# Turning the attended values inside the next batch's first heads, casting the keys' high parts on ScalarE, and sending the queries first

## The chip, the cores and the metric

The kernel runs on one NeuronCore of a Trainium2 chip. The metric is device time in microseconds. A core has TensorE (PE in the profile, its weight loads are PEld), VectorE (DVE), ScalarE (ACT), GpSimd (POOL) and SyncE (SP), which run their own instruction streams in order and meet through semaphores. Matmuls write PSUM, which POOL cannot reach; transposes in the kernel are made either by PE (a matmul against an identity) or by a DMA that SP issues.

## The reference

Tokens of 8 rows of 512 are embedded (three tables summed, then a layer norm), go through one attention layer and one mixture-of-experts layer with a residual around each. The attention is what matters here. For every batch row there are 16 heads; each has three branches: a causal one over compressed keys, one over 128 selected positions, and a window of 128.

```python
q = concatenate([qn, rope(qr)])                 # 32 + 64 wide, 16 heads
o1 = attn(q, k1, v1, causal)                    # latent keys and values
o2 = attn(q, rope(k_selected), v_selected)      # 128 kept positions
o3 = attn(q, rope(k_window), v_window, window)  # the last 128 positions
o  = gate[0] * o1 + gate[1] * o2 + gate[2] * o3
h  = h + concat_heads(o) @ Wproj
```

## The kernel before

The first 200 us embed the tokens, choose the positions and prepare weights; the last 65 us are the experts. Between lies the attention, eight batches of 16 heads. A query tile of a head is 128 positions, so a head has four units, t = 0 to 3. For one unit PE computes the scores of the three branches into one of two PSUM buffers S (`scores`), DVE adds the mask and takes the row maxima (`maxima`, L1029), ACT takes the exponentials (`probs`, L653), PE turns the probabilities into PSUM PT (`turn_probs`, L1402 and L1409), ACT copies them out as fp16 (`take_hi`, L665), DVE makes the rest of the rounding, also fp16 (`take_lo`, L1039), and PE multiplies by the values (`values`, L1424). All products in fp16 are made from a high and a low part, three matmuls for each. The scores run three units ahead of the values. The order on each engine is written out by hand, in a function `turn` on PE (L1441), DVE (L1130) and ACT (L676) that does one head.

Beside this, every head needs its query and keys. PE projects head h+2's query at the start of turn h and head h+3's keys at its end into the one PSUM bank X (`q_proj`, `k_proj`); ACT copies them to `qk` (`evac_q`, `evac_k`). The next use of X waits for that copy. POOL does one `cycle` (L546) a head: `prepare` (L538) waits for both copies, rotates query and key together (L437, L438, L440, L441), casts the key to fp16 (L469), takes its rest (L472), casts the query (L458), takes its rest (L461); then come the rest of the next head's values (`low_values`, L492, whose high part ACT casts in `high_values`, L642) and the sum of the three branches of the head before (`branch_sum`, L485 and L487), which goes to `o_b`. There is one `qparts` and one `kparts`. SP turns each by a DMA transpose into `qh` and `kh`, the keys first (`turn_keys` L317, `turn_queries` L326), when they are split and the scores that read the old ones are done. PE waits for both, of head h+1, ahead of the scores of unit t = 1 of turn h; these are head h+1's first.

The last two heads of a batch prepare the next batch's first two heads (the other order of POOL is at the end of its block, after `heads`). Between batches stands `behind`, on each engine (ACT L729, DVE L1175, PE L1493): the last value projections, the first three scores, and what is left of the batch before. For that PE waits for the last `branch_sum`, turns `o_b` in four groups of four 128 x 128 blocks into PT (`attended`, L1500), and ACT and DVE copy two groups each to `oT` (L594, L1168). The projection with `Wproj` (`project_rows`, L1429) and the residual (`half_residual`, L1124) then stand in units 1 and 2 of the next batch's heads 0 and 1 and use X; the next key projection waits for the residual. The last batch has no `behind`; its values are turned ahead of the experts. During the last batch POOL also normalises rows for the experts in every second cycle (L507 to L512).

Of the kernel before, what the change touches and what calls it, by code (L numbers as in the profile page):

```python
# [5 lines left out]
B, T, C = 8, 512, 64  # L6
P = 128
# [25 lines left out]
def tower(nc, d, out):  # L33
# [5 lines left out]
    with ctx:  # L39
# [217 lines left out]
        def _(sp):  # L257
# [94 lines left out]
            for hp in range(NH // 2 - 1):  # L352
                turn_keys(0, (B - 1) * NH + hp * 2 + 2)
                turn_queries(0, (B - 1) * NH + hp * 2 + 2)
                sp.wait_ge(s["xn_row"], hp + 2)
                sp.dma_start(xn_all[:, hp * NT * C:(hp + 1) * NT * C].rearrange("p (t c) -> p t c", t=NT), xn_b[:]).then_inc(s["xn_kept"], 16)
                turn_keys(1, (B - 1) * NH + hp * 2 + 3)
                turn_queries(1, (B - 1) * NH + hp * 2 + 3)
# [13 lines left out]
        def _(g):  # L372
# [90 lines left out]
            def split_key(par, b, hh, turned):  # L463
                H = b * NH + hh
                g.wait_ge(s["rope"], turned)
                g.nop(nofuse=True)
                g.wait_ge(s["k_turned"], H * 16 + 16)
                g.nop(nofuse=True)
                g.tensor_copy(kparts[:, 0, :, NOPE:P], kk[par][:, :, NOPE:P]).then_inc(s["k_high"], 1)  # L469
                g.wait_ge(s["k_high"], H + 1)  # L470
                g.nop(nofuse=True)
                g.tensor_tensor(kparts[:, 1, :, NOPE:P], kk[par][:, :, NOPE:P], kparts[:, 0, :, NOPE:P], ALU.subtract).then_inc(s["k_split"], 1)  # L472
# [65 lines left out]
            def prepare(par, b, hh, x):  # L538

                n = rope_count(b, hh, None)  # L540
                g.wait_ge(s["x_evac"], x + 2)
                rope(qk[par], rt9, cos9, sin9, n)
                split_key(par, b, hh, n)
                split_query(par, b, hh, n)

            def cycle(b, h, par, rows=None, add=True):  # L546
# [45 lines left out]
        def _(act):  # L592
# [44 lines left out]
            def evac_k(par, x, H=None):  # L637
                if H is not None:
                    act.wait_ge(s["k_split"], H)
                evac(kk[par][:, :, NOPE:P], X[:, 0:5 * HD].rearrange("p (t q) -> p t q", t=5), x)  # L640

            def high_values(par, b, hh):  # L642
                act.wait_ge(s["pv_done"], (b * NH + hh) * NT - 2)
                copy(vh[par][:, 0, :, 0:VD], vall[:, :, ds(hh * VD, VD)]).then_inc(s["v_high"], 1)
# [30 lines left out]

            def turn(b, h, xb, p, last, nxt=None, rows=None, more=True):  # L676
# [52 lines left out]
            def behind(b, nxt, U, first):  # L729

                def attended(c):
                    act.wait_ge(s["oT_psum"], (b - 1) * 4 + c + 1)
                    copy(oT[:, c, :], PT[:, 0:512]).then_inc(s["oT_act"], 1)
# [6 lines left out]
                if not first:  # L740
                    attended(0)
                probs(0, 0, b, U)
                lead(LEAD.index("kp2"), nxt, b * NH)
                if not first:
                    attended(2)
                probs(1, 1, b, U + 1)
                take_hi(0, 0, U)
                probs(2, 2, b, U + 2)
# [7 lines left out]
            def heads(b, rows=False):  # L756
                with act.Fori(0, NH // 2 - 2) as hp:
                    for p in range(2):
# [57 lines left out]
        def _(dve):  # L816
# [312 lines left out]

            def turn(b, H, p, last, nxt=None, rows=None, back=None):  # L1130

                U = H * NT
                for t in range(NT):
# [41 lines left out]
            def behind(b, U, first):  # L1175
                value(b, 7)
                if not first:
                    attended(b - 1, 1)
                maxima(0, 0, U)
                if not first:  # L1180
                    attended(b - 1, 3)
                maxima(1, 1, U + 1)
# [11 lines left out]
            def heads(b, rows=False):  # L1194
                for p in range(2):
                    turn(b, b * NH + p, p, 0, rows=0 if rows and p == 0 else None, back=b - 1 if b > 0 else None)
                with dve.Fori(1, NH // 2 - 1) as hp:
                    turn(b, b * NH + hp * 2, 0, 0, rows=hp if rows else None)
                    turn(b, b * NH + hp * 2 + 1, 1, 0)
# [51 lines left out]
        def _(pe):  # L1251
# [160 lines left out]
            def values(u, t, p, U, first):  # L1412
# [14 lines left out]
                last.then_inc(s["pv_done"], 1)  # L1427

            def project_rows(b, t, x):  # L1429

# [9 lines left out]

            def turn(h, H, xb, p, last, b=None, nxt=None, rows=None, back=None, more=True):  # L1441


                U = H * NT
                for t in range(NT):
                    u = p * NT + t
                    if last < 1 and t == 0:
                        q_proj(h + 2, xb + x_index(0, "qp"))
                    if back is not None and t in (1, 2):
                        project_rows(back, p * 2 + t - 1, xb + 1)  # L1450
                    if back is not None and t == 3:
                        pe.wait_ge(s["h_done"], back * 2 + p + 1)
# [40 lines left out]
            def behind(b, nxt, H, first):  # L1493


                def attended(c):
                    if c >= 2:
                        pe.wait_ge(s[["oT_act", "oT_dve"][c % 2]], (b - 1) * 2 + 1)
                    for t in range(NT):
                        last = tp(PT[:, (c % 2) * 512 + t * P:(c % 2) * 512 + (t + 1) * P], o_b[:, t, c * P:(c + 1) * P], ident)  # L1500
                    last.then_inc(s["oT_psum"], 1)

                for j in range(6, 9):
                    value(b, j)
                if not first:
                    pe.wait_ge(s["osum_done"], H + 2)
                    pe.wait_ge(s["pT_sb"], 2 * H * NT + 2)
                    attended(0)
                    attended(1)
                pe.wait_ge(s["v_act"], b * 5 + 5)  # L1510
# [4 lines left out]
                lead("kp2", b, nxt)  # L1515
                if not first:
                    attended(2)
                    attended(3)
                scores(1, 1, 0, H * NT + 1)
                scores(2, 2, 0, H * NT + 2)  # L1520
                if not first:
                    pe.wait_ge(s["oT_act"], b * 2)
                    pe.wait_ge(s["oT_dve"], b * 2)
                turn_probs(0, 0, H * NT)
# [11 lines left out]
            def heads(b, rows=False):  # L1536
                for p in range(2):
# [205 lines left out]
```

## Time and profile before

| | |
|---|---|
| median of 3 runs | 1754.34 us (1753.4 to 1754.41) |
| the profiled execution | 1754.28 us, span 1752.5 us |
| busy: PE, DVE, ACT, POOL | 1365.7, 1399.5, 1209.9, 1362.3 us |
| granted clock of TensorE, mean | 0.964 of full speed |
| DMA transposes | 128 of queries, 128 of keys |

The rest of the time of an engine is idle: waiting for a semaphore or for its next instruction. The share of busy time is an average over the whole span. In the views below a row of a timeline gives the start, the duration, the engine, the line, the operation, output and inputs by the program's names, the shape and the count merged into the row; in brackets stands how long the engine was idle just before and what ended that. Instructions that follow each other at once overlap by some hundredths of a microsecond.

### The profile page before, as it was taken

To read this page: it belongs to the slowest core of one execution; us is meant where nothing else is said; L and a number is where in the kernel's file an instruction comes from. 1 tells how busy PE (TensorE), PEld (TensorE's weight loads), DVE (VectorE), ACT (ScalarE), POOL (GpSimd) and SP (SyncE) were. 2 spreads that over 40 slices of the span, in tenths; PEclk is the share of its full clock that TensorE was granted. 3 is DMA by queue.
4 is the path that set the end of the run, shared out by engine and by line. 5 is a ranking of instruction groups with operands and counts; after the bars stand their busy time and mean duration, and the time that the engine had idled before them with its cause. 6 is when DMAs were issued, how large, how long until landed. Compare 5 with 4: busy or idle time off the path is not lost.

```text
span 1752.5 us, 61262 instructions
## 1 busy us (share of the span) xinstructions
PE 1365.7 (78%) x19368; PEld 1140.4 (65%) x19368; DVE 1399.5 (80%) x4989; ACT 1209.9 (69%) x3280; POOL 1362.3 (78%) x1680
## 2 busy tenths in 40 slices
PE   1042388889888988888888888888888888888788
PEld 0021277777777777777777777777777777777643
DVE  4756678888888888878887888878888888888835
ACT  0032178877787788778887788778877887777634
POOL 6775578977897789779987898789877997899510
PEclk9986599999999999999999999999999999999989
DMA  5110133223332323232233233332333332333200
GB/s 99 23 26 6 30 73 54 54 48 69 56 64 48 66 55 61 55 67 55 54 57 63 53 64 55 59 55 54 55 62 52 64 58 42 64 66 69 57 4 22
DMA packets 327657, 93.59 MB, mean 53 GB/s; under 512 B 321104, under 2 KB 323024, under 8 KB 327520
## 3 DMA queue, kind: packets, MB, share of 16 engines
q1 hardware_dynamic: 324448, 88.61, 27.2%
q0 software_dynamic: 3072, 3.15, 1.1%
q8 instruction: 85, 1.39, 0.3%
q14 instruction: 52, 0.43, 0.1%
HBM read 6.64 MB, written 1.05 MB: 4 GB/s over the span
## 4 chain that ended last, share of the span: by engine, by line
POOL 51%; issue 23%; DVE 10%; PE 9%; DMA 3%; POOLq 2%; ACT 2%; DVEq 0%; ACTq 0%; SPq 0%
POOL big L438 9%; POOL big L437 8%; POOL big L398 6%; POOL qk L440 5%; POOL qk L441 5%; POOL vh L492 4%; POOL kparts L469 4%; POOL qparts L458 4%; DVE S L1029 3%; POOL osum L485 2%; PE S L1377 2%; DMA kh<-kparts 2%; POOL o_b L487 2%; DVE big L1039 1%; POOL kparts L472 1%
## 5 line engine op out<-in xcount | busy, mean ns | idle before, releaser
L653 ACT ACTIVATE big<-S,negm 128x128 f32<-128x128 f32 (+3 forms) x1536 | 575.6, 448 | 196.2 <-DVE negm L1029 195.6
L1039 DVE SCALAR_TENSOR_TENSOR big<-PT,big 128x384 f16<-128x384 f32 (+3 forms) x1024 | 471.3, 499 | 17.1 <-ACT big L665 11.4
L665 ACT ACTIVATE big<-PT 128x384 f16<-128x384 f32 (+3 forms) x1024 | 417.3, 458 | 90.1 <-PE PT L1402 67.6
L1029 DVE CUSTOM_DVE_ANT_0 S<-S,mask_c,unscale 128x128 f32<-128x128 f32 (+3 forms) x512 | 284.7, 556 | 160.9 <-PE S L1377 157.3
L1377 PE MATMUL S<-k1T,qh 128*128 128x128 f16 (+3 forms) x1536 | 294.9, 301 | 141.0 <-DMA qh<-qparts 101.3
L1377 PE MATMUL S<-kh,qh 128*128 128x128 f16 (+1 forms) x3072 | 320.0, 241 | 0.0
L1424 PEld LDWEIGHTS O<-vh,big 128*128 128x128 f16 x8064 | 273.7, 96 | 22.9 <-issue 6.3
L1424 PE MATMUL O<-vh,big 128*128 128x33 f16 x8064 | 283.1, 178 | 4.4 <-issue 3.9
L437 POOL TENSOR_TENSOR big<-qk,cst 128x576 f32<-128x576 f32 (+2 forms) x144 | 182.5, 1267 | 104.9 <-ACT qk L594 103.1
L1377 PEld LDWEIGHTS S<-kh,qh 128*128 128x128 f16 x3072 | 227.3, 99 | 55.2
L1409 PE MATMUL PT<-cst,big 128*128 128x128 f32 x1408 | 244.5, 278 | 2.7 <-DVE big L1039 2.6
L1402 PE MATMUL PT<-cst,big 128*128 128x128 f32 x1280 | 230.7, 279 | 17.0 <-DVE big L1039 16.4
L1377 PEld LDWEIGHTS S<-k1T,qh 128*128 128x128 f16 x1536 | 116.0, 98 | 180.9 <-issue 126.5
L1029 DVE CUSTOM_DVE_ANT_0 S<-S,cst,kfix 128x256 f32<-128x256 f32 (+1 forms) x512 | 231.9, 453 | 0.0
L1029 DVE DVE_READ_ACCUMULATOR2_ANT negm<- 128x1 f32 x1536 | 215.4, 140 | 0.2
L1029 DVE CUSTOM_DVE_ANT_0 S<-S,mask_c,kfix 128x128 f32<-128x128 f32 x512 | 180.9, 353 | 0.1
L1409 PEld LDWEIGHTS PT<-cst,big 128*128 128x128 f32 x1408 | 164.4, 143 | 15.9 <-issue 10.0
L1402 PEld LDWEIGHTS PT<-cst,big 128*128 128x128 f32 x1280 | 151.4, 143 | 32.0 <-issue 14.7
L461 POOL TENSOR_TENSOR qparts<-qk,qparts 128x512 f16<-128x512 f32 x128 | 148.2, 1158 | 18.6
L594 ACT ACTIVATE qk<-X 128x480 f32<-128x480 f32 (+1 forms) x256 | 151.8, 593 | 14.5 <-PE X L1324 11.3
L438 POOL TENSOR_TENSOR big<-qk,big 128x576 f32<-128x576 f32 x112 | 157.8, 1409 | 0.0
L472 POOL TENSOR_TENSOR kparts<-qk,kparts 128x480 f16<-128x480 f32 x128 | 140.5, 1097 | 18.6
(296 smaller groups left out, 2092.0 us busy)
## 6 DMA issues: line engine op xcount, KB each, us to landing
lat_b<-lat_all SPq DMA_DIRECT2D x8, 448.0 KB, 3.1
qh<-qparts SPq DMA_TRANSPOSE x128, 3.1
kh<-kparts SPq DMA_TRANSPOSE x128, 3.5
xnT_all<-xnT_b SPq DMA_DIRECT2D x14, 128.0 KB, 2.5
xn_b<-xn_all SPq DMA_DIRECT2D x8, 128.0 KB, 2.8
xnT_b<-xnT_all SPq DMA_DIRECT2D x8, 128.0 KB, 2.7
out_dram<-h_all SPq DMA_DIRECT2D x8, 128.0 KB, 2.0
xn_all<-xn_b SPq DMA_DIRECT2D x7, 128.0 KB, 2.0
```

Of the source, the lines that this page charges most:

```text
L437: g.tensor_tensor(tmp[:, 0], v, cos, ALU.mult)
L438: g.tensor_tensor(tmp[:, 1], v, sin, ALU.mult).then_inc(s["rope_t"], 1)
L472: g.tensor_tensor(kparts[:, 1, :, NOPE:P], kk[par][:, :, NOPE:P], kparts[:, 0, :, NOPE:P], ALU.subtract).then_inc(s["k_split"], 1)
L594: return nc.scalar.activation(dst, src, ACT.Copy)
L653: last = nc.scalar.activation(pr[par][:, lo:lo + n], S[par][:, lo:lo + n], ACT.Exp, bias=negm[par][:, k:k + 1], scale=-1.0)
L665: last = nc.scalar.activation(pT[par][:, 0, lo:lo + n], PT[:, lo:lo + n], ACT.Copy, scale=PSCALE)
L1029: last = v.tensor_tensor_reduce(out=z, in0=z, in1=m, scale=unscale[:] if k == 0 else kfix[:], scalar=3.0e38, op0=ALU.add, op1=ALU.min, acc ...
L1039: v.scalar_tensor_tensor(pT[par][:, 1, lo:lo + n], PT[:, lo:lo + n], PSCALE, pT[par][:, 0, lo:lo + n], ALU.mult, ALU.subtract).then_inc(s[ ...
L1377: last = mm(z[:, lo:lo + n], qh[par][:, c, t * P:(t + 1) * P], keys[:, a, :], start=(c + a == 0), stop=(c == 1))
L1402: last = tp(PT[:, lo:lo + P], src[:, lo:lo + P], ident)
L1409: last = tp(PT[:, lo:lo + P], src[:, lo:lo + P], ident)
L1424: last = mm(o, w[:, c, blocks[i] * P:(blocks[i] + 1) * P], vh[p][:, a, v0 + i, :], start=(j == 0), stop=(j == len(parts) - 1))
```

## The change

Three things are altered.

1. The attended values are no longer turned in `behind`. PE turns group c in units 1 and 2 of the next batch's heads 0 and 1 into X (`attended_rows`), ACT copies the even groups there, after `take_hi` of unit 1, and DVE the odd ones in unit 2; the next key projection waits for DVE's copy. The projection and the residual move on by two heads, to heads 2 and 3. These heads are now written out on PE and DVE (four instead of two), and two on ACT (none before). POOL's last addition of `branch_sum` waits, from the second batch on, until the batch before is turned.
2. In `prepare` POOL no longer casts the key; ACT does (`high_key`), in unit 2 of the turn, after `take_hi`. It waits for POOL's rotation, and POOL's rest of the key waits for the cast. The four heads prepared at the change of batches (two each time) keep the old way. `high_values` on ACT moves from unit 2 to unit 1.
3. POOL splits the query before the key, and SP sends the queries' transpose before the keys'.

```diff
@@ sync
                     for par in range(2):
+                        turn_queries(par, b * NH + hp * 2 + (par + 2))
                         turn_keys(par, b * NH + hp * 2 + (par + 2))
-                        turn_queries(par, b * NH + hp * 2 + (par + 2))
@@ gpsimd
             def branch_sum(par, b, hh):
...
+                if b > 0:
+                    g.nop(nofuse=True)
+                    g.wait_ge(s["oT_psum"], b * 4)
+                    g.nop(nofuse=True)
                 g.tensor_tensor(o_b[:, :, ds(hh * VD, VD)], osum[:], obr[par][:, :, 2, :], ALU.add).then_inc(s["osum_done"], 1)
...
                 rope(qk[par], rt9, cos9, sin9, n)
-                split_key(par, b, hh, n)
                 split_query(par, b, hh, n)
+                low_key(par, b, hh)
@@ scalar
+            def high_key(par, b, hh):
+                H = b * NH + hh
+                act.wait_ge(s["rope"], b * (NH + 2) + hh + 3)
+                act.wait_ge(s["k_turned"], H * 16 + 16)
+                copy(kparts[:, 0, :, NOPE:P], kk[par][:, :, NOPE:P]).then_inc(s["k_high"], 1)
...
-                    if t == 2 and last < 2:
+                    if t == 1 and last < 2:
                         high_values(1 - p, b, h + 1)
...
                         take_hi(u + 1, (t + 1) % NT, U + t + 1, rows)
+                    if back is not None and t == 1:
+                        act.wait_ge(s["oT_psum"], back * 4 + 2 * p + 1)
+                        copy(oT[:, 2 * p, :], X[:, 0:512]).then_inc(s["oT_act"], 1)
+                    if t == 2 and last < 1:
+                        high_key(p, b, h + 2)
@@ vector
-                    if back is not None and t == 2:
+                    if back is not None and t == 2 and early:
+                        dve.wait_ge(s["oT_psum"], back * 4 + 2 * p + 2)
+                        v.tensor_copy(oT[:, 2 * p + 1, :], X[:, 0:512]).then_inc(s["oT_dve"], 1)
+                    if back is not None and t == 2 and not early:
                         half_residual(back, p)
@@ tensor
+            def attended_rows(b, c, x):
+                if c == 0:
+                    pe.wait_ge(s["osum_done"], (b + 1) * NH + 2)
+                if c % 2 == 0:
+                    x_wait(x)
+                if c % 2 == 1:
+                    pe.wait_ge(s["oT_act"], b * 2 + c // 2 + 1)
+                for t in range(NT):
+                    last = tp(X[:, t * P:(t + 1) * P], o_b[:, t, c * P:(c + 1) * P], ident)
+                last.then_inc(s["oT_psum"], 1)
...
-                    if back is not None and t in (1, 2):
+                    if back is not None and early and t in (1, 2):
+                        attended_rows(back, p * 2 + t - 1, xb + 1)
+                    if back is not None and early and t == 3:
+                        pe.wait_ge(s["oT_dve"], back * 2 + p + 1)
+                    if back is not None and not early and t in (1, 2):
                         project_rows(back, p * 2 + t - 1, xb + 1)
...
-                for p in range(2):
-                    turn(p, b * NH + p, xbase(b) + p * 2, p, 0, rows=0 if rows and p == 1 else None, back=b - 1 if b > 0 else None)
-                with pe.Fori(1, NH // 2 - 2) as hp:
+                for h in range(4):
+                    turn(h, b * NH + h, xbase(b) + h * 2, h % 2, 0, rows=h // 2 if rows and h % 2 == 1 else None,
+                         back=b - 1 if b > 0 else None, early=h < 2)
+                with pe.Fori(2, NH // 2 - 2) as hp:
```

The three `attended` functions of `behind` and their calls and waits go.

## Rows read from the trace of the kernel before

**Rows 1.** The page, part 1: busy us, share of span, instructions.

```profile
PE 1365.7 (78%) x19368; PEld 1140.4 (65%) x19368; DVE 1399.5 (80%) x4989; ACT 1209.9 (69%) x3280; POOL 1362.3 (78%) x1680
```

**Rows 2.** Waits, whole span: who waited for whom, us, times, longest.

```profile
POOL big L437 <- ACT qk L594: 103.1, 65, 14.9
PE S L1377 <- DMA qh<-qparts: 101.3, 69, 3.6
```

**Rows 3.** Timeline of POOL, steady heads of the second batch.

```profile
514.07 1.40 POOL L437 TENSOR_TENSOR big<-qk,cst 128x576 f32<-128x576 f32 x1 [0.25 <-ACT qk L594]
...
518.73 0.58 POOL L469 CAST kparts<-qk 128x480 f16<-128x480 f32 x1 [0.27 <-POOL qk L441]
519.45 1.10 POOL L472 TENSOR_TENSOR kparts<-qk,kparts 128x480 f16<-128x480 f32 x1
520.50 0.61 POOL L458 CAST qparts<-qk 128x512 f16<-128x512 f32 x1
521.25 1.16 POOL L461 TENSOR_TENSOR qparts<-qk,qparts 128x512 f16<-128x512 f32 x1
...
524.13 1.40 POOL L437 TENSOR_TENSOR big<-qk,cst 128x576 f32<-128x576 f32 x1
...
534.50 1.40 POOL L437 TENSOR_TENSOR big<-qk,cst 128x576 f32<-128x576 f32 x1 [0.30 <-ACT qk L594]
```

**Rows 4.** Timelines of SP and PE there; last, landing times of all key transposes.

```profile
520.78 1.32 SPq L323 DMA_TRANSPOSE kh<-kparts  x1
522.55 1.23 SPq L332 DMA_TRANSPOSE qh<-qparts  x1
...
525.89 0.34 PE L1377 MATMUL S<-k1T,qh 128*128 128x128 f16 x3 [1.69 <-DMA qh<-qparts]
...
DMA to landing us min/median/max: 3.3/3.5/5.8
```

**Rows 5.** Timeline of POOL: third batch, heads 4 and 14; last batch, a pair.

```profile
609.92 1.40 POOL L437 TENSOR_TENSOR big<-qk,cst 128x576 f32<-128x576 f32 x1 [1.02 <-ACT qk L594]
...
712.07 1.40 POOL L437 TENSOR_TENSOR big<-qk,cst 128x576 f32<-128x576 f32 x1 [0.23 <-ACT qk L594]
...
1510.68 1.41 POOL L437 TENSOR_TENSOR big<-qk,cst 128x576 f32<-128x576 f32 x1 [1.74 <-ACT qk L594]
...
1533.41 1.39 POOL L437 TENSOR_TENSOR big<-qk,cst 128x576 f32<-128x576 f32 x1
```

**Rows 6.** Timeline of ACT, the steady stretch of rows 3.

```profile
516.66 0.88 ACT L665 ACTIVATE big<-PT 128x384 f16<-128x384 f32 x2
...
518.22 0.45 ACT L594 ACTIVATE vh<-vall 128x288 f16 x1
518.62 0.98 ACT L665 ACTIVATE big<-PT 128x512 f16<-128x512 f32 x2
...
522.37 1.20 ACT L653 ACTIVATE big<-S,negm 128x384 f32<-128x384 f32 x3 [0.79 <-DVE negm L1029]
```

**Rows 7.** Timelines of PE, DVE, SP and POOL, from second to third batch.

```profile
579.42 1.09 PE L1500 MATMUL PT<-cst,o_b 128*128 128x128 f32 x8 [1.36 <-POOL o_b L487]
...
587.84 1.08 PE L1437 MATMUL X<-wproj,oT 128*128 128x64 f32 x8
588.76 0.33 PE L1377 MATMUL S<-k1T,qh 128*128 128x128 f16 x3
...
580.55 0.69 DVE L1168 COPY oT<-PT 128x512 f32<-128x512 f32 x1 [2.35 <-PE PT L1500]
...
585.17 1.33 SPq L323 DMA_TRANSPOSE kh<-kparts  x1
...
587.77 1.41 POOL L437 TENSOR_TENSOR big<-qk,cst 128x576 f32<-128x576 f32 x1 [2.86 <-ACT qk L594]
...
598.83 1.41 POOL L437 TENSOR_TENSOR big<-qk,cst 128x576 f32<-128x576 f32 x1 [2.10 <-ACT qk L594]
```

More of the change, by code:

```diff
@@ L542, in prepare @@
                 rope(qk[par], rt9, cos9, sin9, n)
-                split_key(par, b, hh, n)
                 split_query(par, b, hh, n)
+                low_key(par, b, hh)
             def cycle(b, h, par, rows=None, add=True):
@@ L674, in take_hi, with turn @@
                     last.then_inc(s["pT_hi"], 1)
-            def turn(b, h, xb, p, last, nxt=None, rows=None, more=True):
+            def turn(b, h, xb, p, last, nxt=None, rows=None, more=True, back=None):
                 H = b * NH + h
@@ L729, in behind @@
             def behind(b, nxt, U, first):
-                def attended(c):
-                    act.wait_ge(s["oT_psum"], (b - 1) * 4 + c + 1)
-                    copy(oT[:, c, :], PT[:, 0:512]).then_inc(s["oT_act"], 1)
                 value(b, 6)
@@ L739, in behind @@
                 copy(vh[0][:, 0, :, 0:VD], vall[:, :, 0:VD]).then_inc(s["v_high"], 1)
-                if not first:
-                    attended(0)
                 probs(0, 0, b, U)
                 lead(LEAD.index("kp2"), nxt, b * NH)
-                if not first:
-                    attended(2)
                 probs(1, 1, b, U + 1)
@@ L756, in heads @@
             def heads(b, rows=False):
-                with act.Fori(0, NH // 2 - 2) as hp:
+                for p in range(2):
+                    turn(b, p, xbase(b) + p * 2, p, 0, rows=0 if rows and p == 1 else None, back=b - 1 if b > 0 else None)
+                with act.Fori(1, NH // 2 - 2) as hp:
                     for p in range(2):
@@ L1128, in half_residual, with turn @@
                 v.tensor_tensor(hb, X[:, i * 2 * C:(i + 1) * 2 * C], hb, ALU.add).then_inc(s["h_done"], 1)
-            def turn(b, H, p, last, nxt=None, rows=None, back=None):
+            def turn(b, H, p, last, nxt=None, rows=None, back=None, early=False):
                 U = H * NT
@@ L1176, in behind @@
                 value(b, 7)
-                if not first:
-                    attended(b - 1, 1)
                 maxima(0, 0, U)
-                if not first:
-                    attended(b - 1, 3)
                 maxima(1, 1, U + 1)
@@ L1194, in heads @@
             def heads(b, rows=False):
-                for p in range(2):
-                    turn(b, b * NH + p, p, 0, rows=0 if rows and p == 0 else None, back=b - 1 if b > 0 else None)
-                with dve.Fori(1, NH // 2 - 1) as hp:
+                for h in range(4):
+                    turn(b, b * NH + h, h % 2, 0, rows=h // 2 if rows and h % 2 == 0 else None,
+                         back=b - 1 if b > 0 else None, early=h < 2)
+                with dve.Fori(2, NH // 2 - 1) as hp:
                     turn(b, b * NH + hp * 2, 0, 0, rows=hp if rows else None)
@@ L1439, in project_rows, with turn @@
                     last.then_inc(s["attn_psum"], 1)
-            def turn(h, H, xb, p, last, b=None, nxt=None, rows=None, back=None, more=True):
+            def turn(h, H, xb, p, last, b=None, nxt=None, rows=None, back=None, early=False, more=True):
                 U = H * NT
@@ L1448, in turn @@
                         q_proj(h + 2, xb + x_index(0, "qp"))
-                    if back is not None and t in (1, 2):
+                    if back is not None and early and t in (1, 2):
[3 more added lines that the diff above has]
+                    if back is not None and not early and t in (1, 2):
                         project_rows(back, p * 2 + t - 1, xb + 1)
-                    if back is not None and t == 3:
+                    if back is not None and not early and t == 3:
                         pe.wait_ge(s["h_done"], back * 2 + p + 1)
@@ L1493, in behind @@
             def behind(b, nxt, H, first):
[L1496 to L1501, printed above, removed]
                 for j in range(6, 9):
                     value(b, j)
[L1505 to L1509, printed above, removed]
                 pe.wait_ge(s["v_act"], b * 5 + 5)
@@ L1515, in behind @@
                 lead("kp2", b, nxt)
-                if not first:
-                    attended(2)
-                    attended(3)
                 scores(1, 1, 0, H * NT + 1)
                 scores(2, 2, 0, H * NT + 2)
-                if not first:
-                    pe.wait_ge(s["oT_act"], b * 2)
-                    pe.wait_ge(s["oT_dve"], b * 2)
                 turn_probs(0, 0, H * NT)
@@ L1536, in heads @@
             def heads(b, rows=False):
-                for p in range(2):
-                    turn(p, b * NH + p, xbase(b) + p * 2, p, 0, rows=0 if rows and p == 1 else None, back=b - 1 if b > 0 else None)
-                with pe.Fori(1, NH // 2 - 2) as hp:
+                for h in range(4):
+                    turn(h, b * NH + h, xbase(b) + h * 2, h % 2, 0, rows=h // 2 if rows and h % 2 == 1 else None,
+                         back=b - 1 if b > 0 else None, early=h < 2)
+                with pe.Fori(2, NH // 2 - 2) as hp:
                     for p in range(2):
```

6 lines of the change are left out of this document (4 added, 2 removed).

## The prediction

> **What bounds the kernel now.** The page gives four engines about the same busy share: DVE 1399.5 us, PE 1365.7, POOL 1362.3, ACT 1209.9 [rows 1]. So shares don't say who waits for whom; the table of waits comes next. Its two entries that matter are POOL's first multiply of the rotation (L437) waiting for the evacuation of the next queries by ACT, and PE's scores waiting for the transposed queries [rows 2]. Each waits for the other's product, 65 and 69 times. That is a ring, not a pipeline behind one engine.
>
> The timelines of one undisturbed stretch give the ring its lengths. POOL starts on head 12's query and key at 514.07 after an idle 0.25 (it waited for ACT), and on head 14's at 534.50, again after a wait of 0.30 [rows 3]. PE starts the first scores of head 12 at 525.89, having idled 1.69 for the landing of the queries [rows 4]. So
>
> - L, from POOL's start to the scores: 525.89 - 514.07 = 11.82 us (rotation 4.66, key cast and rest, query cast and rest, transposition, landing);
> - R, from the scores to POOL's start two heads later, through PE, DVE and ACT in that order: 534.50 - 525.89 = 8.61 us.
>
> L + R = 20.43 for two heads, 10.2 a head. The stretch from 609.92 to 712.07 [rows 5] has ten heads: 10.2 each. POOL alone could do a head in 524.13 - 514.07 = 10.06 [rows 3]; it is close behind, but not first. About 12 of 16 heads in each of seven batches (84) run like this. In the last batch POOL has the normalisation too, and two heads take 1533.41 - 1510.68 = 22.73 [rows 5]: there POOL sets the pace.
>
> The Trainium skill (Perfetto Trace Analysis, section Identifying the Most-Contended Engine) says to take the engine with the highest occupancy as the bottleneck and to optimise it first. Relieving POOL is in that spirit. The trace speaks against it outside the last batch; what the rule would give is rival A.
>
> **The change, part by part.** All sums are against the profiled execution's own 1754.28 us (span 1752.5 and 1.8 around it), which is 0.06 under the median shown.
>
> *1. Key cast to ACT, queries first: L.* On POOL one head loses 519.45 - 518.73 = 0.72 [rows 3]. L changes otherwise. Now: cast of the key at 4.66, its rest, cast of the query, its rest until 522.41, that is 8.34, issue at 8.48 [rows 3, 4]. After: query cast at 4.66, its rest 0.75 later, ready at 4.66 + 0.75 + 1.16 = 6.57; key rest 1.10 more: 7.67. SP issues the query at 6.57 + 0.23 (520.78 stands 0.23 behind the end of L472), is held 1.23 by it, and takes 0.14 for the next, so the key goes out at 8.17, not 7.9. Its landing takes 3.5 (median) where the queries' took 3.1 or so (525.89 - 522.55 = 3.34 with PE's 0.24) [rows 3, 4]. 8.17 + 3.5 + 0.24 = 11.91: L grows by 0.09. What is late next is the key, the longer transpose, in the queries' place. Bounds: -0.1 (its shortest landing, 3.3) to +0.3 (the two transposes, now 1.4 apart instead of 1.8, hinder each other). I take +0.09.
>
> The high part must be there when POOL reaches it. ACT ends its 512-column copy at 519.60 [rows 6], which is 5.53 after POOL's start and after the rotation (4.4); the cast, about 0.58 by the copies of 288 and 512 columns, ends at 6.2, POOL needs it at 6.6. Covered by 0.4; where something delays ACT at this place by more, POOL, the key's transpose and the scores are late by the rest.
>
> *2. What ACT gets: R.* The added 0.58 stands before the exponentials of a unit; behind these are the next key's evacuation, a copy and the exponentials that end R. ACT idles 0.79 just there, for DVE [rows 6], so it is hidden, by 0.2. The value cast (0.45) moves ahead of the copy at 516.66, before which ACT had no idle time in this head [rows 6]. The copy is what DVE and then PE's next transposes wait for. Bounds: 0 (it falls into idle time) and 0.45. I take 0.2, about half. Evacuating the key 0.6 later makes PE's query projection late, but evacuation of the queries waits for the exponentials anyway.
>
> Steady heads: (0.09 + 0.2)/2 = 0.145 a head, since L and R are shared by two heads; 84 x 0.145 = **+12.2 us**. Bounds (-0.1 + 0)/2 and (0.3 + 0.45)/2: -4 to +31.
>
> *3. Attended values out of the gap between batches.* Now PE idles 1.36 for POOL's last sum and turns 8 blocks (1.09) before the first scores [rows 7]; these go 1.4 us earlier. But the first scores of head 1 stand at 588.76, and its key was issued at 585.17, 3.59 before them [rows 7] (a transpose and PE's 0.24), on a chain that runs on POOL alone from the last heads on. It isn't shortened; two sums with the added wait and its no-operations (0.1 each, from the 0.27 ahead of L469 [rows 3]) lengthen it by 0.2. So the 1.4 us end as idle time at 588.8. What the gap gives is POOL's start on head 2, now after 2.86 idle [rows 7]; nobody waits for it first.
>
> Then the added work lands in R. A quarter of the projection (1.08) or a turning of 4 blocks (0.55, half of the 1.09) [rows 7] stands in each of units 1 and 2 of a head; the one in unit 2 is inside R, with the wait of the key projection behind it. From 588.76 to 598.83 is 10.07, against 8.61: the projection costs 1.46 there, its 1.08 and 0.38 of the wait for DVE's addition [rows 7]. With the turning I take 0.55 + 0.87 = 1.42, as DVE then copies for 0.69 [rows 7] where it adds 128 columns now (bounds of that wait 0.38 and 1.07). With S for first scores, P for POOL's start, both by head:
> before: S1 588.76, P3 598.83, P4 609.92, S3 = P3 + 11.82 = 610.65, P5 619.26, S4 621.74, P6 630.35, S5 = P5 + 11.82 = 631.08.
> after: S1 588.96, P3 = + 10.03 = 598.99, S2 = P3 + 0.39 (one turning of 0.55 in place of the 1.08 with which it was 0.92) = 599.38, P4 609.41, S3 = P3 + 11.82 = 610.81, P5 = + 10.07 = 620.88, S4 = P5 + 0.92 = 621.80, P6 = 631.87, S5 = P5 + 11.82 = 632.70.
> Both strands of the ring are 1.5 to 1.6 late: four heads now pay in R where two did. 7 x 1.55 = **+10.9 us**; bounds 0 (projection halves fall into PE's waits) and +17 (they also make the key's cast late). The wait that the sums get for all turning done is over by 6 us when they come, and costs its no-operations only, which POOL has room for.
>
> *4. Last batch.* POOL's 22.73 becomes 22.73 - 2 x 0.72 + 2 x 0.1 = 21.49; six pairs: -7.4. The ring (20.43 and the rows' work) comes near, so I take **-6 us** (-8 to -1).
>
> *5. Longer straight code* on PE, DVE and ACT means more loading of instructions; landings of up to 5.8 against 3.5 [rows 4] show transposes that something holds up. 0 taken, +7 at most.
>
> Sum 12.2 + 10.9 - 6 = +17.1: 1754.3 + 17.1 = **1771 us**.
>
> **Rivals.**
> A. *POOL sets the pace everywhere.* For it: 10.06 of 10.2, and 1362 us busy. Against it: POOL's waits on ACT, 0.25 and 0.30 in [rows 3]. Price -0.62 x 84 = -52, with part 4 -59: 1695. Below 10.06 nothing follows unless L or R shortens. 7%.
> B. *The gap's gain is kept* (faster): the first scores 1.4 us earlier pass through because the key of head 1 comes in time or heads 2 and 3 absorb the projection in PE's 1.69 idle. Its place is S1; it decides if S1 moves by over 0.7. -10, with part 4 -16, steady heads unchanged: 1738. Against it: the 3.59 us from 585.17 [rows 7]. 13%.
> C. *Nothing to be seen*: steady heads at 0, half of part 3, and part 4 take each other up: 1754. 12%.
> D. *ACT becomes the bound*: the value cast costs its whole 0.45, key casts are late: +31 + 11 - 6: 1790. 13%.
> The forecast with its own range (1759 to 1783) has 55%.
>
> A difference of over 0.2% (3.5 us) can be told from none: faster 20%, same 12%, slower 68%. The range, 1740 to 1790, takes in B nearly and D, and leaves A out.
>
> **What will show it.** Right: PE's scores wait for kh<-kparts instead of qh<-qparts; POOL's wait on ACT (now 103.1) grows by some 0.6 a head while its busy time falls by 60 us; ten steady heads take 103 to 104 us; the first scores of head 1 still follow the key's landing; POOL's start on heads 5 and 6 comes later behind S1 by 1.5; last-batch pairs near 21.5. Wrong: POOL without idle time before L437, ten heads in under 101, or S1 more than a microsecond nearer to the start of its batch.

## The result and the profile after

| | before | after |
|---|---|---|
| median | 1754.38 us | 1807.03 us (4 runs, 1801.75 to 1811.11) |
| profiled execution, span | 1754.28, 1752.5 us | 1811.11, 1809.0 us |
| mean granted clock | 0.964 | 0.953 |

The ratio is 1.030 (1.0267 to 1.0334). The forecast was 1771 us, range 1740 to 1790: the sign is right, but the loss foreseen is a third of what came, and the time lies above the range. Some executions of most kernels lie 40 to 50 us above the rest and ratios leave these out on both sides; the one profile here that is of such an execution (the run with half of the turnings left out) spends its added time at the lower clock behind 1707 us, after the attention, so that its heads can be compared.

The first part of the page after. POOL has 62.5 us less work than in [rows 1], the kernel takes 53 us more.

```profile
PE 1415.4 (78%) x19368; PEld 1160.5 (64%) x19368; DVE 1407.7 (78%) x4989; ACT 1262.0 (70%) x3392; POOL 1299.8 (72%) x1568
```

Waits, whole span (us, times, longest), beside [rows 2]: the keys stand in the queries' place in PE's wait, POOL waits more for ACT, and there is a new wait of POOL for the cast key.

```profile
POOL big L437 <- ACT qk L602: 164.6, 114, 14.9
PE S L1390 <- DMA kh<-kparts: 102.8, 95, 3.7
POOL kparts L476 <- ACT kparts L602: 60.6, 34, 5.2
```

POOL's timeline in a steady stretch of the fifth batch, for [rows 3, 5]. Four heads take 1100.31 - 1058.61 = 41.70, 10.42 each, where they took 10.2. POOL's time that became free is idle time ahead of L437: 0.98 a head, where [rows 3] has 0.25, nothing and 0.30.

```profile
1058.61 1.41 POOL L437 TENSOR_TENSOR big<-qk,cst 128x576 f32<-128x576 f32 x1 [0.97 <-ACT qk L602]
...
1063.27 0.61 POOL L458 CAST qparts<-qk 128x512 f16<-128x512 f32 x1 [0.28 <-POOL qk L441]
1064.03 1.16 POOL L461 TENSOR_TENSOR qparts<-qk,qparts 128x512 f16<-128x512 f32 x1
1065.15 1.11 POOL L476 TENSOR_TENSOR kparts<-qk,kparts 128x480 f16<-128x480 f32 x1
...
1079.45 1.40 POOL L437 TENSOR_TENSOR big<-qk,cst 128x576 f32<-128x576 f32 x1 [0.98 <-ACT qk L602]
...
1100.31 1.41 POOL L437 TENSOR_TENSOR big<-qk,cst 128x576 f32<-128x576 f32 x1 [0.98 <-ACT qk L602]
```

SP and PE there, for [rows 4]: the key goes out at 1066.80, 8.19 behind POOL's start (8.17 was worked out), and the scores start at 1070.28, 11.67 behind it. PE's scores follow the key's landing.

```profile
1065.42 1.23 SPq L332 DMA_TRANSPOSE qh<-qparts  x1
...
1066.80 1.37 SPq L323 DMA_TRANSPOSE kh<-kparts  x1
...
1070.28 0.34 PE L1390 MATMUL S<-k1T,qh 128*128 128x128 f16 x3 [0.82 <-DMA kh<-kparts]
```

The first heads of the third batch, for [rows 7], all engines. PE turns group 0 early, idles 2.14 for head 1's key and starts its scores (S1) at 602.28. The second turning waits 0.70 for ACT's copy, the key projection for DVE's. POOL has the query ready by 606 but waits 5.07 for ACT's key cast, which stands behind a copy ahead of which ACT itself idles 2.93.

```profile
599.51 0.63 PE L1451 MATMUL X<-cst,o_b 128*128 128x128 f32 x4 [0.47 <-ACT qk L602]
...
602.28 0.41 PE L1390 MATMUL S<-k1T,qh 128*128 128x128 f16 x3 [2.14 <-DMA kh<-kparts]
...
605.74 1.12 PE L1451 MATMUL X<-cst,o_b 128*128 128x128 f32 x4 [0.70 <-ACT oT L602]
...
609.40 0.98 ACT L679 ACTIVATE big<-PT 128x512 f16<-128x512 f32 x2 [2.93 <-issue]
...
610.26 0.61 ACT L602 ACTIVATE kparts<-qk 128x480 f16<-128x480 f32 x1
...
610.52 0.50 PE L1346 MATMUL X<-wkw,xh 128*128 128x96 f16 x8 [0.42 <-DVE oT L1160]
...
611.01 1.10 POOL L476 TENSOR_TENSOR kparts<-qk,kparts 128x480 f16<-128x480 f32 x1 [5.07 <-ACT kparts L602]
...
615.40 1.41 POOL L437 TENSOR_TENSOR big<-qk,cst 128x576 f32<-128x576 f32 x1 [2.63 <-ACT qk L602]
```

POOL starts on head 3 at 615.40, 13.12 behind S1; before it was 10.07 [rows 7], predicted 10.03. The stretches show the other half of why. Columns: stretch, length, busy time (instructions) of PE, its loads, DVE, ACT, POOL, granted clock, DMA share, GB/s. Just behind the idle time TensorE runs at its lower level, 1.2 GHz, for 7 us.

```profile
599.40:602.20 2.80, 0.63 (x4) 0.42 (x4) 1.26 (x6) 2.20 (x6) 2.75 (x2) 1.00 0.83 195
602.20:609.20 7.00, 6.22 (x48) 5.68 (x49) 2.67 (x11) 2.25 (x6) 3.32 (x5) 0.51 0.43 110
609.20:615.30 6.10, 5.68 (x98) 4.97 (x97) 5.23 (x19) 5.22 (x14) 1.77 (x2) 1.00 0.37 57
```

Where the time lies, by the ends of ACT's evacuation of the queries, mean of batches 1 to 6 (counted from 0), in us:

| stretch of a batch | before | after | only part 1 | parts 2 and 3 |
|---|---|---|---|---|
| heads 0 to 2 | 29.4 | 27.8 | 27.8 | 29.3 |
| heads 2 to 8 | 65.0 | 72.9 | 71.3 | 64.9 |
| heads 8 to 14 | 61.2 | 62.7 | 61.2 | 62.5 |
| head 14 to the next batch | 24.2 | 25.5 | 24.4 | 24.7 |

Most of the loss is in heads 2 to 8, and part 1 brings it. Parts 2 and 3 cost heads 8 to 14 1.3 a batch and heads 2 to 8 nothing: there even the kernel before takes 10.8 a head and not 10.2, so the plain ring of the prediction holds for some 8 heads of a batch and not for 12.

### The profile page after: what moved, and what is told of

Read it like the earlier page. It is cut to its first block and busy times, and to the rows that moved or that the text cites. A ratio compares the mean times of both kernels' runs of the same rounds, so it can differ in the third digit from the quotient of the medians.

```text
span 1809.0 us, 60454 instructions
## 1 busy us (share of the span) xinstructions
PE 1415.4 (78%) x19368; PEld 1160.5 (64%) x19368; DVE 1407.7 (78%) x4989; ACT 1262.0 (70%) x3392; POOL 1299.8 (72%) x1568
## 5 line engine op out<-in xcount | busy, mean ns | idle before, releaser
L1390 PE MATMUL S<-kh,qh 128*128 128x128 f16 (+1 forms) x3072 | 325.5, 243 | 0.0
L437 POOL TENSOR_TENSOR big<-qk,cst 128x576 f32<-128x576 f32 (+2 forms) x144 | 182.6, 1268 | 164.9 <-ACT qk L602 164.6
L1437 PEld LDWEIGHTS O<-vh,big 128*128 128x128 f16 x8064 | 278.0, 96 | 19.4 <-issue 6.3
L1390 PEld LDWEIGHTS S<-kh,qh 128*128 128x128 f16 x3072 | 231.3, 100 | 56.3
L1415 PE MATMUL PT<-cst,big 128*128 128x128 f32 x1280 | 238.2, 286 | 25.8 <-DVE big L1052 24.7
L1422 PE MATMUL PT<-cst,big 128*128 128x128 f32 x1408 | 248.3, 281 | 2.2 <-DVE big L1052 1.4
L1415 PEld LDWEIGHTS PT<-cst,big 128*128 128x128 f32 x1280 | 153.4, 146 | 56.1 <-DVE big L1052 31.7
L1422 PEld LDWEIGHTS PT<-cst,big 128*128 128x128 f32 x1408 | 166.9, 145 | 22.6 <-issue 12.1
```

The lines of the kernel that those rows point to most:

```text
L437: g.tensor_tensor(tmp[:, 0], v, cos, ALU.mult)
L1390: last = mm(z[:, lo:lo + n], qh[par][:, c, t * P:(t + 1) * P], keys[:, a, :], start=(c + a == 0), stop=(c == 1))
L1415: last = tp(PT[:, lo:lo + P], src[:, lo:lo + P], ident)
L1422: last = tp(PT[:, lo:lo + P], src[:, lo:lo + P], ident)
L1437: last = mm(o, w[:, c, blocks[i] * P:(blocks[i] + 1) * P], vh[p][:, a, v0 + i, :], start=(j == 0), stop=(j == len(parts) - 1))
```

## Experiments

Ratios are to the kernel before, with their 95% intervals; 0.001 is 1.75 us. L (from POOL's start on a head to its first scores) and R (from there to POOL's start two heads on) are the prediction's; here both are read from the ends of ACT's evacuation of the queries (POOL starts some 0.3 behind).

### Only the attended values moved

```diff
  # kernel before, with the change's part 1 alone; POOL casts the key, keys sent first
-                if not first: attended(...)        # behind, on PE, ACT and DVE
...
+                        attended_rows(back, p * 2 + t - 1, xb + 1)
```

> The kernel before with part 1 alone: attended values turned in heads 0 and 1, projection in heads 2 and 3, the loops written out as in the changed kernel; POOL casts the key, keys go first, value cast in unit 2. Theory 1 (TensorE's clock): the early scores leave PE idle by 2 us ahead of head 1's first scores, the granted clock halves there for 3.4 or 6.8 us in most batches, and that is what the heads 2 to 7 lose: most of the loss is here, 1785 to 1795 us, with ten or more stretches at half clock between 400 and 1550 us. Theory 2 (the key cast on ACT comes late): without the cast on ACT the heads 2 to 7 of a batch lose only the 1.6 us of my sum: 1762 to 1768 us, and few stretches at half clock. Steady heads stay at 10.2 us under both.

1787.69 us, ratio 1.0192 (1.0146 to 1.0239): +33.7 us. The steady heads are as before. Heads 0 to 2 gain 1.6 us a batch, heads 2 to 8 lose 6.3. The time is the one that goes with theory 1, but the attention has 8 stretches at half clock, not ten or more, and the next run shows that they are not the bulk of the loss.

### The same, with PE kept busy while it waits for head 1's key

```diff
+                            if back is not None and early and p == 0:
+                                for _ in range(18):
+                                    mm(O[:, 416:512], k1T[:, 0, 0:P], k1T[:, 0, 0:96], start=True, stop=True)
                             pe.wait_ge(s["k_turned"], H * 16 + 48)
```

> The kernel attended with 18 matmuls of 96 columns that nobody reads, written to unused columns of O, on PE in head 0 ahead of its wait for head 1's key (1.5 to 1.9 us of idle time there in attended). They add work and shorten nothing. Theory 1 (the idle stretch halves the granted clock and that costs the time): no stretch at half clock behind the change of batches any more (seven batches, 3.4 to 10.2 us each in attended), heads 2 to 8 come down from 70 to 72 us to 65 to 67: 1760 to 1770 us. Rival (projection and turning in R alone cost it, the clock is a consequence): 1785 to 1795 us, as attended or a little over.

1782.01 us, 1.0165 (1.0140 to 1.0191): 4.7 us less by the ratios, though the intervals overlap; that is nearer to the rival's time than to theory 1's. The idle time ahead of S1 falls to 1.11, and the stretch behind it keeps the full clock. One batch of each kernel, first with only the values moved, behind a gap of 1.87 (S1 at 958.5):

```profile
958.40:961.80 3.40, 2.85 (x30) 2.68 (x30) 1.62 (x8) 1.18 (x3) 2.98 (x5) 0.50 0.50 148
```

and with the added matmuls (S1 at 589.38):

```profile
589.38 0.34 PE L1388 MATMUL S<-k1T,qh 128*128 128x128 f16 x3 [1.11 <-DMA kh<-kparts]
```

```profile
592.00:599.00 7.00, 6.14 (x96) 5.43 (x97) 4.72 (x19) 4.56 (x13) 3.48 (x4) 1.00 0.47 87
```

So the clock may be part of it, some 5 us, but no more: with all seven of these idle times at 0.96 to 1.39 and none of them followed by half clock, 29 of the 34 us stay.

### The first heads written out, nothing moved

```diff
-                for p in range(2):
-                    turn(p, b * NH + p, xbase(b) + p * 2, p, 0, ...)
-                with pe.Fori(1, NH // 2 - 2) as hp:
+                for h in range(4):
+                    turn(h, b * NH + h, xbase(b) + h * 2, h % 2, 0, ...)
+                with pe.Fori(2, NH // 2 - 2) as hp:
...  # the same two heads more on DVE, and heads 0 and 1 on ACT
```

> The kernel before with heads 2 and 3 written out on PE and DVE and heads 0 and 1 on ACT, and nothing moved: 18 or so more loads of instructions. If instruction loads that hit the transposes are a large part of the loss of attended: 1765 to 1775 us, with waits of PE of 2 to 3.5 us and half clock behind them. If they are the small term of my step 5 (0 taken, 7 at most): 1752 to 1761 us.

1761.39 us, 1.0029 (1.0014 to 1.0045): +5.1 us for straight code alone. The page counts 103 instruction loads on the DMA queues instead of 85. In one stretch of the DMA view (822 to 832 us) such a load stands beside a query transpose that lands after 5.4 us, and PE idles 3.91, 2.2 us more than in [rows 4]. Queue, packets, MB; issues with the median landing; then PE:

```profile
q8 instruction: 1, 0.02, 0.7%
...
kh<-kparts SPq DMA_TRANSPOSE x2, 3.5
qh<-qparts SPq DMA_TRANSPOSE x1, 5.4
```

```profile
828.24 0.34 PE L1380 MATMUL S<-k1T,qh 128*128 128x128 f16 x3 [3.91 <-DMA qh<-qparts]
```

No run isolates the load, but the fourteen traces bear it out. Of their transposes issued between 200 and 1700 us, 2724 have no instruction load that begins within 3 us of their issue, and 28 of these land over 1 us behind the median of their kind (3.1 and 3.5); of the 858 that have one, 311 do. All 28 have a load that begins later, before they land. The Trainium skill (Runtime: NRT & Kernel Launch, Instruction fetch mechanics) calls the cost of such a load mostly hidden and full unrolling preferred; this kernel measures +5.1 us for it.

### Half of the turnings left out

```diff
-                    if back is not None and early and t in (1, 2):
-                        attended_rows(back, p * 2 + t - 1, xb + 1)
+                    if back is not None and early and t == 1:
+                        attended_rows(back, p * 2, xb + 1)
...  # DVE copies the turning that is there a second time
```

> Only the attended values are moved, as in the run 'attended' (1787.7 us), but the odd groups c = 1 and 3 are not turned: their 8 turnings a batch are left out, and VectorE copies the even group a second time. With them goes PE's wait in unit 2 for ScalarE's copy out of X. Theory (the step R from a head's first scores to POOL's start two heads on grew through the second turning, 0.55 us, and its wait of about 0.87 us for ScalarE, where the prediction had counted one copy only): R of the two turning heads falls from about 11.4 to about 10 us, 1.4 us a batch or a little more on each strand, 7 batches: about 1777 us. Rival (the moved work costs nothing there, the loss is instruction loads and the lower clock, which this leaves as they are): 1785 to 1789 us.

1776.73 us, 1.0122 (1.0104 to 1.0140): 12.3 us less than with all of them, with intervals apart. The same place in both, head 2's first scores to the evacuation of head 4's queries, PE and ACT. First with all turnings: 602.99 to 614.53, R = 11.54.

```profile
602.99 0.33 PE L1388 MATMUL S<-k1T,qh 128*128 128x128 f16 x3
...
605.50 0.62 ACT L602 ACTIVATE oT<-X 128x512 f32<-128x512 f32 x1
...
606.18 0.66 PE L1449 MATMUL X<-cst,o_b 128*128 128x128 f32 x4 [0.87 <-ACT oT L602]
...
606.67 0.49 PE L1388 MATMUL S<-k1T,qh 128*128 128x256 f16 x3
...
609.73 0.50 PE L1344 MATMUL X<-wkw,xh 128*128 128x96 f16 x8 [0.86 <-DVE oT L1158]
...
613.92 0.61 ACT L602 ACTIVATE qk<-X 128x512 f32<-128x512 f32 x1
```

With the second left out: 602.83 to 612.85, R = 10.02.

```profile
602.83 0.33 PE L1389 MATMUL S<-k1T,qh 128*128 128x128 f16 x3
...
605.00 0.49 PE L1389 MATMUL S<-k1T,qh 128*128 128x256 f16 x3
...
608.05 0.50 PE L1345 MATMUL X<-wkw,xh 128*128 128x96 f16 x8 [0.78 <-DVE oT L1159]
...
612.24 0.61 ACT L602 ACTIVATE qk<-X 128x512 f32<-128x512 f32 x1
```

The second turning costs 1.5 us of R: 606.67 - 602.99 = 3.68 against 605.00 - 602.83 = 2.17 to the next scores, of which 0.87 is the wait for ACT to empty X.

### The keys' part: cast by ACT, queries first, nothing else moved

```diff
+                    if t == 2 and last < 1:
+                        high_key(p, b, h + 2)
...
-                    if t == 2 and last < 2:
+                    if t == 1 and last < 2:
                         high_values(1 - p, b, h + 1)
```

> The kernel before with parts 2 and 3 alone: key cast on ACT in unit 2, value cast in unit 1, queries split and sent first; attended values stay between the batches. Both theories: steady heads at 10.42 us as in the changed kernel (R longer by 0.47, L shorter by 0.1). Theory 1: no idle 2 us ahead of head 1's first scores, so few stretches at half clock, 84 heads x 0.22 = +18 and a last batch unchanged: 1768 to 1775 us. Theory 2: key casts late in the heads behind the change of batches, because ACT does the projection's neighbours there: 1780 to 1795 us.

1768.57 us, 1.0100 (1.0061 to 1.0140). L is 11.81 (before 11.90), R 9.02 (8.50), medians over the steady heads.

### The same, with the cast of the values left in unit 2

> As keys, but the value cast of ACT stays in unit 2. If the value cast ahead of the copy of unit 1 is what lengthens R (my step 2), R comes back to 8.5 to 8.6, steady heads take 10.15 to 10.2 and the kernel 1745 to 1756 us, now with a shorter L. If it is the key cast ahead of the exponentials of unit 2, R stays at 9.0 and the time is that of keys.

1748.22 us, 0.9965 (0.9952 to 0.9977), faster than before; L 11.83, R 8.51. Measured again:

> The same kernel as keys_hv2, measured again in more rounds, since it stood only 0.35% under the kernel before. If that was the edit, 1746 to 1750 us; if it was chance, within 0.1% of the kernel before, 1753 to 1756 us.

1750.36 us, 0.9968 (0.9955 to 0.9981). The gain is small and real, and in the profiles it shows in the last batch only, where POOL sets the pace: from head 0's to head 15's evacuation that takes 173.6 and 173.3 us in the two profiles against 178.1, while batches 1 to 6 together are no shorter (1080.7 and 1082.4 against 1078.7). One line takes the gain to a loss of 1%. Its way through the engines, a steady head of the third batch in each, counted from the first scores: first with the values cast in unit 2.

```profile
674.57 0.34 PE L1389 MATMUL S<-k1T,qh 128*128 128x128 f16 x3 [1.13 <-DMA kh<-kparts]
...
675.67 0.87 ACT L675 ACTIVATE big<-PT 128x384 f16<-128x384 f32 x2
...
676.21 1.01 DVE L1051 SCALAR_TENSOR_TENSOR big<-PT,big 128x384 f16<-128x384 f32 x2
...
676.94 0.60 PE L1414 MATMUL PT<-cst,big 128*128 128x128 f32 x4
...
677.63 0.98 ACT L675 ACTIVATE big<-PT 128x512 f16<-128x512 f32 x2
...
682.46 0.61 ACT L598 ACTIVATE qk<-X 128x512 f32<-128x512 f32 x1
```

Cast in unit 1:

```profile
678.32 0.34 PE L1389 MATMUL S<-k1T,qh 128*128 128x128 f16 x3 [1.05 <-DMA kh<-kparts]
...
679.46 0.45 ACT L598 ACTIVATE vh<-vall 128x288 f16 x1
...
679.79 0.88 ACT L675 ACTIVATE big<-PT 128x384 f16<-128x384 f32 x2
...
680.32 1.02 DVE L1051 SCALAR_TENSOR_TENSOR big<-PT,big 128x384 f16<-128x384 f32 x2 [0.22 <-ACT big L675]
...
680.93 0.66 PE L1414 MATMUL PT<-cst,big 128*128 128x128 f32 x4
...
681.69 0.98 ACT L675 ACTIVATE big<-PT 128x512 f16<-128x512 f32 x2 [0.24 <-PE PT L1414]
...
686.58 0.61 ACT L598 ACTIVATE qk<-X 128x512 f32<-128x512 f32 x1
```

ACT's copy starts 1.47 behind the scores instead of 1.10, DVE's 2.00 (with a wait of 0.22 for it) instead of 1.64, PE's next transposes 2.61 instead of 2.37, ACT's next copy 3.37 instead of 3.06 (now waiting for PE), and the queries' evacuation 8.26 instead of 7.89. The cast goes round PE and DVE once and comes back to ACT as idle time. This head shows 0.37 of it; over the steady heads the median R grows by 0.51.

### Only the cast of the values moved

> The kernel before with one line moved: ScalarE casts the next head's values in unit 1 instead of unit 2. Theory (this alone lengthens R by its whole 0.5 us, as keys against keys_hv2 suggests: R 9.02 against 8.51): 84 heads x 0.25 = +21 us, about 1775 us. Rival (it costs only where ScalarE has the key's cast as well): R 8.5, 1754 to 1757 us.

1765.28 us, 1.0052 (1.0029 to 1.0076); R 8.64. Neither expectation is right: alone it costs R 0.14, with the key's cast behind it 0.5. The profiles show a reason, idle time of ACT ahead of the copy that the cast now precedes. In the kernel before, ACT idled 0.3 to 0.4 there in 18 of 42 steady heads (heads 6 to 11 of the first seven batches), as in this one; with the key's cast on ACT and the value cast left in unit 2, it idles there over 0.1 in 1 of 42 (4 in the second measurement).

```profile
506.61 0.87 ACT L665 ACTIVATE big<-PT 128x384 f16<-128x384 f32 x2 [0.39 <-PE PT L1402]
```

So the copy starts 1.25 behind the scores instead of 1.11 (medians) with the value cast alone ahead of it, and 1.62 with the key's cast on ACT as well: the key's cast uses up the idle time that hid the rest.

### Only the order changed: queries split and sent first

```diff
-                split_key(par, b, hh, n)
                 split_query(par, b, hh, n)
+                split_key(par, b, hh, n)
```

> The kernel before with the queries split and sent first and nothing else; POOL casts both, the key last. By the working of L the key is then split 0.72 later than in the changed kernel, at 8.39 behind POOL's start, and lands 3.4 to 3.5 later: L 12.0 to 12.1 against 11.82, R unchanged: 10.3 us a steady head, +0.1 x 84 = +8: 1760 to 1766 us. If the order of the two transposes costs nothing, 1754.

1765.29 us, 1.0052 (1.0036 to 1.0068); L 12.05 (11.90), R unchanged. The order alone costs 0.15 of L, 6.3 us over 84 heads; with the key's cast on ACT this comes back (11.83). The rest of the 9 us is open: the profile has 8 stretches at half clock in the attention where the kernel before has 4.

### The change, with the cast of the values back in unit 2

```diff
-                    if t == 1 and last < 2:
+                    if t == 2 and last < 2:
                         high_values(1 - p, b, h + 1)
```

> The changed kernel with the value cast of ACT back in unit 2. keys_hv2 against keys gave 20 us for this edit, and R came back from 9.02 to 8.51. If the parts add up, 1807 - 20 = 1787 us, and steady heads at 10.2 us; if the front of a batch has its own limit (the key cast on ACT late behind PE's half clock), less is given back there: 1787 to 1795.

1786.45 us, 1.0181 (1.0153 to 1.0209): 20.6 us less than the change, the same as the 20.3 between the two kernels above. With the 18 unread matmuls of above added:

> after_hv2 with the 18 unread matmuls of attended_busy. Theory 1: it returns the same as there (some 20 us) and is then the nearest that attended values in heads 0 and 1 come to the kernel before: 1760 to 1770 us. Rival (the clock is a consequence): as after_hv2. Theory 2 in what is left of it (key cast on ACT tied to the scores of head 1): a wait of POOL's key rest on ACT's cast stays at 3 us or more in head 0 even at full clock.

Only two executions can be compared, 1775.39 and 1776.54 us against 1781.99 to 1788.90. That is in line with some 8 us for the clock, but too few for an interval.

### Projection ahead of the scores

```diff
  # the faster kernel of above (values cast in unit 2)
-                    if back is not None and t in (1, 2):
-                        project_rows(back, p * 2 + t - 1, xb + 1)
+                    if back is not None and t == 1:
+                        project_rows(back, p * 2, xb + 1)
+                        project_rows(back, p * 2 + 1, xb + 1)
```

> keys_hv2 (key cast on ScalarE, queries first, value cast left in unit 2: 1748.2 us) with both quarters of a head's projection in unit 1, ahead of the scores of the next head, where PE otherwise idles for the transposed keys; before, the second stands in unit 2, between the scores and ScalarE's and POOL's next work. Theory (what stands in R costs its whole length, what stands before the wait for the keys is partly hidden): first scores of head 1 up to 1.1 us later, R of the two projecting heads 1.1 to 1.5 us shorter, head 2's first scores not later; 0 to 1.4 us a batch gained: 1738 to 1748 us. Rival (the quarter's 1.08 us is paid ahead of the first scores and the wait for DVE's addition remains in R): 1752 to 1756 us.

1748.40 us, 0.9949 (0.9932 to 0.9966). The interval overlaps that of the kernel without it (0.9955 to 0.9981), so it can't be told from nothing. In the profile R of the two projecting heads is 9.08 instead of 10.02, and S1, the first scores of head 1, comes 0.9 later: what leaves R stands ahead of S1 instead. Both beat the kernel before.

## Why the prediction was wrong

The parts add: +33.7 for the values, +17.5 for the keys' part, 51.2 together, against 52.6 measured for the change (0.030 x 1754). Two steps of the sum failed: step 3, which left out a wait for ACT's copy out of X and had no term for the clock, and step 2, which took the value cast at under half of its cost.

**Step 1, L.** Foreseen +0.09. The working was right (key issued 8.19 behind POOL's start, 8.17 foreseen), the landing was a little shorter: the median L is 11.84, 0.06 less than before. Right within its bounds.

**Step 2, R.** Foreseen +0.2 with 0.45 as the end of the range; measured +0.5. This is a term of the sum that was mis-sized: at 84 heads 0.25 would be 21 us instead of 8.4. The 84 was wrong the other way: only about 8 heads of a batch run as the plain ring, and the profile of the keys' part alone loses 1.7 a batch over batches 1 to 6. ACT's key cast, which I had called hidden by 0.2, costs nothing (R 8.51 against 8.50). The value cast, for which I took half although ACT had no idle time there in the head looked at, costs all of it. The bound was wrong as well: it had not counted that ACT, DVE and PE hand this unit round, so that a delay comes back as a wait of ACT for PE.

**Step 3, front of the batch.** S1 was placed right: 602.28 is 30.65 behind the evacuation of head 0's query, and it was 30.4 before. The reason too: the key of head 1 ends its wait. What I had not followed is that PE, having turned earlier, now idles 2.14 there, and comes out of it at the lower clock. R with a turning in it, foreseen as 10.03, is 11.54 at full clock for head 2 and 10.85 for head 1; the run with half of the turnings has 10.02 and 9.4. The working had *one* copy out of X behind the turnings (DVE's, 0.86 measured, 0.87 foreseen) and forgot the other: two turnings of one head share X, so the second waits for ACT's copy of the first. R with the projection was right (10.07 foreseen; 10.0 to 10.3 over the batches). Foreseen +10.9 us, measured +33.7, of which by the ratios:

- the second turning and its wait for ACT: 12.3 us;
- the clock behind the gap: about 5 us (overlapping intervals);
- straight code: 5.1 us, step 5's 0 with +7 as its end;
- 11 or so are left by difference, which no run isolates; that it is about what the step had in it does not confirm the step.

These were measured one by one and need not add exactly. In the change itself one more wait shows: while PE is slow, ACT's copy comes late, its key cast behind it, and POOL, the key's transposition and the scores of the next strand wait (5.07 us above). The prediction had named that wait ("where something delays ACT at this place by more") and covered it by 0.4. It adds little to the time: with the value cast back in unit 2 the change (1.0181, 1.0153 to 1.0209) is no slower than part 1 alone (1.0192). What it can have taken is the 6 us that the keys' part gains by itself, of which 2 are left.

**Step 4, last batch.** Foreseen -1.24 a pair, 6 us in all. In the profiles the last batch, from head 0's to head 15's evacuation, got longer, 179.6 instead of 178.1: its first heads pay for the turnings as in every batch. Its last three pairs took 67.2 / 3 = 22.4 instead of 68.0 / 3 = 22.7. With the values cast in unit 2 and nothing turned it was 65.3 / 3 = 21.8. So POOL's relief is worth 0.9 a pair by itself, and with the value cast in unit 1 most of it is lost. In the profile of the keys' part alone POOL waits 0.65 a pair there for the cast key and 0.4 to 0.7 for the evacuated queries; with the value cast in unit 2 it waits 0.3 to 0.8 for the first and hardly at all for the second. A wait of the change:

```profile
1576.83 1.09 POOL L476 TENSOR_TENSOR kparts<-qk,kparts 128x480 f16<-128x480 f32 x1 [0.91 <-ACT kparts L602]
```

**Rivals.** POOL as the pace (A) is out before the last batch: it idles ahead of 68 of the 112 L437 of full width in the kernel before, and 60 us less work on it, with the value cast left in place, bought 6 us, which the profiles show in the last batch only. The Trainium skill's rule (Perfetto Trace Analysis, Identifying the Most-Contended Engine), to optimise the engine of highest occupancy first, is borne out in the last batch only. In a steady stretch (640 to 701 us) that engine is POOL too, 55.4 us busy of 61.0 against DVE's 53.6, and with 0.6 a head less on it batches 1 to 6 are no shorter. The gap's gain (B) is there, 1.6 us a batch, and is lost more than three times over in the next six heads. Its sign, S1, did not move. One half of D (the value cast costs its whole 0.45) is what happened, with 13%; it was put in as an outer case though its condition, no idle time ahead of the copy, stood in [rows 6] for that head. Its late key casts happened at the front of the batches and cost little, and L did not grow by D's 0.3. The range ended at D's price with my own middle values for all else, so two mis-sized terms in one direction were outside it.

## What to carry to other kernels

In a ring of waits a piece of work costs by its place, not by its engine's idle share: the same 0.45 us cast on ScalarE was worth 20 us between two places one unit apart, and 9 us where ScalarE had less other work. Whether there is idle time at a place is read from many heads, not from one. When a buffer with one holder gets a second use in the same turn, write down each release it now has to wait for, the copy that empties it among them. And when work is taken out of the time ahead of a wait, look at what the engine does in it instead: an idle TensorE can come out of the wait slower.

## What the runs showed of the hardware

In the attention the kernel before had 4 stretches at a granted clock of 0.50 (13.7 us), the change 14 with 58.0 us; a stretch was 3.4, 6.8 or 10.2 us long. The length of PE's idle time alone did not decide: of the kernel before's 41 idle times over 1.45 us in the attention, 4 were followed by such a stretch, of the change's 16, 13 were. Ahead of the first scores of head 1, 19 of the 28 idle times of 1.5 to 3.9 us in four kernels with the moved turnings had one in them or behind them; with the added matmuls none of 7 had (0.96 to 1.39 us), and in the changed kernel with them 2 of 7 (1.27 and 2.79).

Two more heads of straight code, with eighteen more instruction loads, cost 5 us in a kernel that waits for DMA transposes. In the fourteen traces 311 of 858 transposes with an instruction load close behind their issue landed over 1 us late, against 28 of 2724 without.
